# A transformer decoder layer: two of three last products of a self-attention slot moved behind the next slot's scores, eleven identity products at the front, input loaded in eight pieces

## The reference

```python
q = (x @ wq.T).reshape(b, s, N_HEADS, HEAD_DIM)
k = (x @ wk.T).reshape(b, s, N_HEADS, HEAD_DIM)
v = (x @ wv.T).reshape(b, s, N_HEADS, HEAD_DIM)
scores = jnp.einsum('bihd,bjhd->bhij', q, k) * scale
scores = jnp.where(mask[None, None, :, :], -jnp.inf, scores)
attn = jax.nn.softmax(scores, axis=-1)
out = jnp.einsum('bhij,bjhd->bihd', attn, v).reshape(b, s, d)
return out @ wo.T
...
x = _layernorm(x + _L0_attn_ref(x, ...), axis=-1)
```

## Time and profile before

| | us |
|---|---|
| median of 3 runs | 1063.21 |
| lowest and highest of them | 1061.88, 1064.4 |
| the profiled execution, its own time | 1066.47 |
| its span, first to last instruction | 1064.7 |
| PE busy in the span | 1019.2 (96%) |
| DVE, ACT, POOL busy | 704.2, 524.1, 530.5 |

### The profile page before, as it was taken

How to read it: one execution, slowest core, us unless ns; L and a number is a source line. 1 busy time by engine, 2 the same in 40 slices (tenths; PEclk the granted TensorE clock), 3 DMA queues, 4 the chain that set the end, 5 groups by cost and what they waited for, 6 DMA issues and landing times.

```text
span 1064.7 us, 20098 instructions
## 1 busy us (share of the span) xinstructions
PE 1019.2 (96%) x6978; PEld 905.5 (85%) x6978; DVE 704.2 (66%) x1454; ACT 524.1 (49%) x1033; POOL 530.5 (50%) x515
## 2 busy tenths in 40 slices
PE   6999888999999999999999999999999899999996
PEld 5866667899999999999999999999887788778785
DVE  4277776777777777767767767767786364455447
ACT  5355545555455455455455455455543245556510
POOL 0156866763643643643643644644572644454452
PEclk9999999999999999999999999999999999999999
DMA  8100104424323223233223333224210869999742
GB/s 294 60 31 2 60 16 138 150 111 149 120 111 115 98 109 114 97 108 114 99 107 114 101 107 112 101 107 150 93 69 1 333 253 370 395 380 380 279 134 83
DMA packets 44696, 153.45 MB, mean 144 GB/s; under 512 B 3704, under 2 KB 3704, under 8 KB 41568
## 3 DMA queue, kind: packets, MB, share of 16 engines
q1 hardware_dynamic: 42400, 145.38, 38.2%
q0 software_dynamic: 2240, 7.34, 2.1%
HBM read 130.04 MB, written 22.66 MB: 143 GB/s over the span
## 4 chain that ended last, share of the span: by engine, by line
PE 71%; POOL 4%; DVE 4%; issue 3%; ACT 1%; another core or an unknown queue 1%; POOLq 0%; DVEq 0%; ACTq 0%
PE xa_y_ps L86 6%; PE xa_y_ps L88 5%; PE xa_y_ps L87 5%; PE ex_raw_ey_ps L2092 5%; PE ex_raw_gu_ps L86 4%; PE ex_raw_gu_ps L88 4%; PE ex_raw_gu_ps L87 4%; PE xa_c_ps L1880 4%; PE xa_c_ps L1876 3%; PE xa_c_ps L1875 3%; PE xa_turn_ps L1957 3%; PE xa_turn_ps L1913 3%; PE front_k_ps L86 3%; PE front_k_ps L88 3%; PE front_k_ps L87 3%
## 5 line engine op out<-in xcount | busy, mean ns | idle before, releaser
L1221 POOL TENSOR_TENSOR xa_probs<-xa_probs,xa_inv_sum 112x750 f32<-112x750 f32 x63 | 97.9, 1553 | 75.6 <-DVE xa_inv_sum L1548 75.6
L1497 DVE TENSOR_TENSOR xa_kT_lo<-xa_turn_ps,xa_kT_hi 128x750 fp32r<-128x750 f32 x63 | 59.2, 940 | 99.9 <-ACT xa_kT_hi L1309 99.8
L1206 POOL TENSOR_TENSOR k_ms<-k_ss,sum_eps 125x6 f32<-125x6 f32 x63 | 12.6, 200 | 210.7 <-DVE k_ss L1513 210.7
L1875 PE MATMUL xa_c_ps<-xa_probsT_hi,xa_nat 125*128 125x224 f32 x384 | 92.3, 274 | 2.7 <-ACT xa_probsT_hi L1325 2.7
L1876 PE MATMUL xa_c_ps<-xa_probsT_hi,xa_nat 125*128 125x224 f32 x384 | 92.3, 275 | 0.0
L1209 POOL TENSOR_TENSOR k_inv<-k_ms,neg_half 125x6 f32<-125x6 f32 x63 | 83.5, 1326 | 8.3 <-POOL k_ms L1206 6.7
L1325 ACT CAST xa_probsT_hi<-xa_turn_ps 125x672 fp32r<-125x672 f32 x62 | 44.6, 720 | 87.2 <-PE xa_turn_ps L1957 87.2
L1331 ACT ACTIVATE xa_probs<-xa_scores_ps,xa_bias,xa_q_scale 112x375 f32<-112x375 f32 x126 | 82.8, 663 | 5.8 <-DVE xa_bias L1523 4.4
L1875 PEld LDWEIGHTS xa_c_ps<-xa_probsT_hi,xa_nat 125*128 125x128 f32 x384 | 73.6, 192 | 3.5 <-issue 3.1
L1876 PEld LDWEIGHTS xa_c_ps<-xa_probsT_hi,xa_nat 125*128 125x128 f32 x384 | 73.5, 191 | 0.5
L86 PE MATMUL front_k_ps<-land_xa_wk_hi,land_xa_ctx 128*125 128x256 f32 x252 | 71.4, 283 | 1.4 <-DVE front_k_hat L1540 1.0
(11 more groups left out here) (379 smaller groups left out, 3484.9 us busy)
## 6 DMA issues: line engine op xcount, KB each, us to landing
xa_nat<-ctx_split SPq DMA_DIRECT2D x56, 750.0 KB
ex_raw_raw<-in_w_units SPq DMA_DIRECT2D x15, 1408.0 KB, 7.9
ex_raw_raw<-in_w_units SPq DMA_DIRECT2D x15, 768.0 KB
land_ex_raw<-in_w_units SPq DMA_DIRECT2D x8, 1408.0 KB, 8.2
land_ex_raw<-in_w_units SPq DMA_DIRECT2D x8, 768.0 KB, 7.6
ctx_split<-xa_nat SPq DMA_DIRECT2D x8, 750.0 KB
sorted_x<-ex_raw_y_sb SPq DMA_DIRECT2D x7, 768.0 KB, 10.5
ex_raw_x_nat<-sorted_x SPq DMA_DIRECT2D x21, 256.0 KB, 8.3
```

What stands on the lines that cost most here:

```text
L1221: pool.tensor_tensor(probs[0:T, u % 2], probs[0:T, u % 2], inv_sum[0:T, u % 2, :].unsqueeze(2).broadcast_to([T, 2, KV]), ALU.mult).then_in ...
L1497: dve.tensor_tensor(kT_lo[:, :, 0:KV], turn_ps[:, :, 0:KV], kT_hi[:, :, 0:KV].bitcast(F32), ALU.subtract).then_inc(sem["kT_lo_done"], 1)
L1875: pe.matmul(c_view[:, c], nat[0:KT, u % 2, 0, at], probsT_hi[0:KT, :, cols], start=(t == 0), stop=False)
```

## The change

It has four parts. First, PE waits for the constants at its very start and issues eleven matmuls of the identity with itself into `y_ps`, plain 32-bit matmuls of 128 by 128, whose result nobody reads. Second, the input arrives in eight transfers, half a chunk each, with a semaphore for each, and ACT waits for halves. Third, in slots 8 to 30 except those with `s % 4 == 3` (18 slots) `output_product` is cut: only its first matmul stays in its place, and the other two are issued behind the scores of the next slot, ahead of its `outputs`. Fourth, in slots 11, 15, 19 and 23 the same is done with the one chunk of `values` that is made there. Within a moved pair the order of the two matmuls is also exchanged.

```diff
+            def first_values(b):
+                wait(pe, "v_copied", b)
+                wait(pe, "turn_lo", b - 4)
+                cols = slice(b * T, (b + 1) * T)
+                pe.matmul(proj_ps[0:T, :], xT_hi[:, 0, cols], wv_hi[:, 0, :], start=True, stop=False)
+            def rest_of_first_values(b):
+                cols = slice(b * T, (b + 1) * T)
+                pe.matmul(proj_ps[0:T, :], xT_hi[:, 0, cols], wv_lo[:, 0, :], start=False, stop=False)
+                pe.matmul(proj_ps[0:T, :], xT_lo[:, 0, cols], wv_hi[:, 0, :], start=False, stop=False)
+            wait(pe, "consts_set", 8)
+            for _ in range(11):
+                pe.matmul(y_ps[:, 0:P], ident[:], ident[:], start=True, stop=True)
...
             for c in range(DC):
-                sp.dma_start(xT_raw[:, c, :], xT[:, c, :]).then_inc(sem[f"xT_{c}_loaded"], 16)
+                for g in range(2):
+                    cols = slice(g * HT, (g + 1) * HT)
+                    sp.dma_start(xT_raw[:, c, cols], xT[:, c, cols]).then_inc(sem[f"xT_{c}_{g}_loaded"], 16)
...
+            def split_output(s):
+                return s - 4 >= QUADS and s % QUADS < QUADS - 1
+            def split_values(s):
+                made = values_in(s)
+                return s >= 4 * QUADS - 5 and made is not None and tuple(made[1]) == (0,)
             for s in range(N):
                 scores(s)
+                if split_output(s - 1):
+                    rest_of_output_product(s - 5)
+                if split_values(s - 1):
+                    rest_of_first_values(values_in(s - 1)[0])
                 if s >= 3:
                     outputs(s - 3)
...
-                if made is not None:
+                if split_values(s):
+                    first_values(made[0])
+                elif made is not None:
                     values(*made)
-                if u >= QUADS and s % QUADS < QUADS - 1:
-                    output_product(u)
+                if split_output(s):
+                    first_output_product(u)
```

More of the change, by code:

```diff
@@ L251, in self_attention @@
         names += [f"{w}_{what}" for w in ("wq", "wk") for what in ("0_loaded", "1_loaded", "hi_done", "lo_done")]
-        names += [f"{array}_{c}_loaded" for array in ("wv", "xT") for c in range(DC)]
+        names += [f"wv_{c}_loaded" for c in range(DC)] + [f"xT_{c}_{g}_loaded" for c in range(DC) for g in range(2)]
         sem = {n: es.enter_context(nc.semaphore("sa_" + n)) for n in names}
@@ L469, in _ @@
             for c in range(DC):
-                wait(act, f"xT_{c}_loaded", 16)
                 for g in range(2):
                     cols = slice(g * HT, (g + 1) * HT)
+                    wait(act, f"xT_{c}_{g}_loaded", 16)
                     act.copy(xT_hi[:, c, cols], xT_raw[:, c, cols]).then_inc(sem["xT_hi_done"], 1)
@@ L741, in _ @@
             values(0, range(DC))
-            wait(pe, "consts_set", 8)
             def scores(u):
@@ L785, in output_product, with first_output_product, rest_of_output_product @@
                                wo_part(qk_lo, q), q == 0, q == QUADS - 1).then_inc(sem["y_ready"], 1)
+            def first_output_product(u):
+                b, q = divmod(u, QUADS)
+                t = b - 1
+                wait(pe, "wo_lo_done", q + 1)
+                wait(pe, "oT_lo_done", u + 1)
+                if q == 0:
+                    wait(pe, "y_added", t)
+                    wait(pe, "proj_copied", len(PROJ))
+                pe.matmul(y_ps[:], oT_hi[:, q, tile_cols(t)], wo_part(qk_hi, q), start=(q == 0), stop=False)
+            def rest_of_output_product(u):
+                b, q = divmod(u, QUADS)
+                cols = tile_cols(b - 1)
+                pe.matmul(y_ps[:], oT_hi[:, q, cols], wo_part(qk_lo, q), start=False, stop=False)
+                pe.matmul(y_ps[:], oT_lo[:, q, cols], wo_part(qk_hi, q), start=False, stop=False).then_inc(sem["y_ready"], 1)
             def first_keys(tiles):
```

## The result

The changed kernel takes 1056.86 us (median, 1055.65 to 1057.8) against 1063.68 (1061.88 to 1064.4) for the kernel before on the same chip: ratio 0.9933, 95% interval 0.9919 to 0.9946, so 5.7 to 8.6 us faster (6.8 by the medians). The prediction was 1057.7 in 1054.8 to 1060.6, with the slots at 3.05, the clock at 1.5 and the start at 1.0.

The account below looks back on a forecast made before the run. PE, busy 96% of the span, was taken as the bound, with DVE nearer from slot 27; slots 3.05, clock 1.5 and start 1.0 sum to 5.55 us, taking the median 1063.21 to 1057.7, range 1054.8 to 1060.6.

Parts of the forecast that it names:

- the slots: Self-attention slots 8 to 30: 22 moved pairs gain 2.58 + 0.22 + 0.25 = 3.05 us together.
- the clock: Front: identity products raise PE's clock before the first projections, nine products at 0.20 instead of 0.37; 1.5 us.
- the start: Front: PE's first real product starts at 7.9 in place of 8.97, taken as 1.0 us.
- The slot's arithmetic: PE-bound slots: a moved pair saves 0.46 ahead of the transposes, costs 0.35 behind the scores, net 0.11 per slot.
- the bubble: Between a slot's scores and outputs: PE idles for ACT's copy of the transposed probabilities, 0.69 - 0.39 = 0.30 us per slot.
- Slot 24: Transposes wait for POOL's scaling, behind a weight's low part: nothing won in slots 23 and 24, wait longer by some 0.5.
- The pieces: Input in eight half chunks: the first half seen at 6.5, 1.1 earlier, with the whole chunk's landing delay; taken as 1.0.
- 1.26 idle is harmless: Ahead of the first keys, 144.91: after 1.26 idle PE continued at the high level, so 1.0 idle at the front should.
- Rival 1: Front: the clock is not high at the first real product; gain 4.05, time 1059.2, chance 0.12.
- Rival 2: All slots: POOL or DVE takes over, PE waits ahead of the transposes; gain 3.1, time 1060.1, chance 0.14.
- Rivals 3 and 4: Slots: switches cost less, 0.16 not 0.35, 1054.7, chance 0.12; or more, 0.85 per pair, 1067.8, chance 0.05.
- The end: Late in the program: the clock falls or not in an idle stretch, which shifted starts may tip by up to 1.6 us.

Follow-up runs that it names:

- the pair behind the outputs: Changed kernel with the moved pair issued behind the outputs instead of between scores and outputs; ratio 0.9961 to the kernel before.
- the last kernel: Changed kernel with POOL's low part of the query weights halved, one half in slot 23, one ahead of slot 27's shift; ratio 0.9908 to before.
- the pieces alone: Kernel before with only the input in eight pieces, no identity products, all triples uncut; ratio 0.9987.
- all three and the halves: Changed kernel with all three last products behind the scores and POOL's query-weight low part halved, slots 23 and 28; ratio 0.9926 to before.
- the pairs alone: Kernel before with only the 22 moved pairs, no identity products, input in four pieces; ratio 0.9971.
- the front alone: Kernel before with only the eleven identity products and the eight input pieces, all triples uncut; ratio 0.9979.
- six products: Changed kernel with six identity products at the front in place of eleven; ratio 0.9959 to the kernel before.

## Why the prediction was right

The time, 0.8 below the forecast, came out for the reasons given, with two terms mis-sized and one step wrong in a way that cost nothing. As a gain it is 6.8 against 5.55, 1.3 more than forecast. The traces say where 1.0 of it lies: slots 0.71 and start 0.54 above their terms, clock 0.25 below.

- **The slot's arithmetic** held to a hundredth: outputs 1.05 behind the scores (1.04), 0.36 paid there (0.35), 0.10 net per slot (0.11), 2.20 per slot (2.2). That the pair pays because it fills the bubble is shown by the kernel with the pair behind the outputs.
- **The slots' sum** was 3.76, not 3.05. Slots 8 to 22 gave 3.11 instead of 2.58; slots 23 and 24 together -0.06 (0), 25 and 26 0.36 (0.22), 27 to 29 0.00 (0), slot 30 0.36 (0.25). The missing part is in slots 14, 18, 22 and 26, which hold the transposes of a block. They gained 0.24 to 0.27 where 0.11 was counted, since outputs to transposes (L129) takes 0.33 now where it took 0.49. The count had treated these slots as all others. What the 0.16 was stands in the row of the weight load (PEld), which comes ahead of the transposes' matmul. In slot 14 before, and in the waits from 69 to 142 us:

```profile
89.07 0.42 PEld L129 LDWEIGHTS sa_proj_ps<-ident,resid 128*128 128x128 f32 x4 [0.33 <-ACT sa_V L465]
```

```profile
PEld sa_proj_ps L129 <- ACT sa_V L465: 1.3, 4, 0.3
```

The block's transposes go into the bank of the values and wait for ACT to copy these out. They come later behind a pair, and the changed kernel has no such wait from 66 to 139 us. Slots 15 and 19, which were worked out apart, gained 0.46 and 0.43 (0.40).
- **Slot 24** did what was said: the wait grew by 0.59 (about 0.5), and nothing was won in 23 and 24. POOL's weights as its cause are shown by the last kernel.
- **The pieces** (1.0) are the mis-sized term: the start gained 1.54, and alone they bring 2.60. The step that failed was that half the chunk would be seen 1.1 earlier, with the landing delay of the whole. ACT saw it 1.64 earlier (5.96) there and 2.60 earlier with the pieces alone (5.00); the other traces with pieces have 5.41 to 5.99. So a half doesn't land with the delay of the whole, and its time differs between executions by up to 1 us (that of a whole chunk by 0.3: 7.60, 7.62, 7.91). Why isn't settled, and the 2.60 of the pieces alone is the best of eleven traces. The Trainium skill's wish for transfers of 1 MiB or more (DMA: Bandwidth & Descriptors, Bandwidth) would have spoken against the cut; here the cut won.
- **The clock** (1.5) gave 1.25. The step "rises at about 6.2, identity products end at 7.0, 1.0 idle" is wrong: they were spaced 0.21 to the end, the low level, and held PE until 7.43. There was no idle time. In other traces with the same front the level rose between 6.0 (pair behind the outputs) and 8.2 (all three and the halves), so 6.2 is inside what happens, and it was taken as if fixed. That the term came near is in part luck: the kernel before had the shortest time to the high level of all traces without identity products, the changed one a long one. Against the pairs alone, which had 6.01, the front brings slot 8 not 2.79 but 4.00 earlier. That 1.26 idle is harmless held in the trace it was read from and not in that of the front alone.
- **Rival 1** (clock not high in time) is what six products do, at 1.34. **Rival 2** showed only in slot 24. **Rivals 3 and 4** fell with the measured 0.36: new changes of size cost as the old ones. (Rival 3's 16 slots count 15 and 19 among those that pay in full, against the sum's own 0.06; without them it is 2.7.)
- **The end** of the profiled execution before, with PE's 2.45 idle and the low clock, was named as what may tip, and did: some 3.5 us between the two profiled runs, of which a low stretch of the changed kernel at 776 took 1.6 back. They are 8.6 apart where the medians are 6.8 apart; the slots and the front explain 6.55.

## What to carry to other kernels

Look for an idle bit that comes once per iteration and is too short to list high in any single wait (0.23 us, 21 times). Moving work into it gains only what is left when its changes between small and large products are paid, and one place further back it gains nothing. Before moving a POOL operation into an idle stretch, look at which DVE instruction runs there: two reads of SBUF on DVE against a POOL read make one of them wait for the other. Work that warms PE up has to last until the clock is near its high level (six products that ended 1.50 us ahead of the work bought nothing), and should end when the real operands are there. Before two gains are said not to add, cut the trace where they are made: one low stretch behind them can hide both.

## What the runs showed of the hardware

- How long PE stays at the low level from its first product on differs between executions of equal fronts: 3.42 us before (to the first product spaced 0.20, the tenth), 6.01 with the pairs alone (8.98 to 14.99, the seventeenth). So the front is worth 2.79 at slot 8 in one pair of traces and 4.00 in another.
- The length of an idle stretch alone doesn't tell whether the clock falls behind it. 1.76 us behind the identity products and 1.26 ahead of the first keys were followed by the high level in their traces; 1.25 at that same place in the front alone, and 0.90 and 0.43 close together at 774 to 776 of the changed kernel, were followed by 3.4 us at the low one, which began 1.8 us behind the end of the 1.25 and of the 0.90. What decides it no run shows.
- The clock column of the windows doesn't show this: for 9.00 to 12.40 of the kernel before, where products come 0.37 apart, it reads 1.00, while behind the idle time near the end it reads 0.51 for products 0.43 apart. At the front only the spacing tells the level.

```profile
9.00:12.40 3.40, 3.40 (x10) 3.04 (x11) 3.29 (x7) 3.26 (x7) 0.00 (x0) 1.00 1.02 344
...
1046.80:1050.00 3.20, 3.12 (x8) 2.49 (x9) 2.79 (x7) 0.00 (x0) 1.34 (x4) 0.51 0.00 0
```

- DVE and POOL lock each other out in either direction: 2.68 us instead of 0.93 for DVE when POOL began first, 1.63 instead of 0.93 for POOL when DVE did.
